# Two transformer layers on one core: who copies the finished attention products, and the order of the head groups

## The reference

```
q = split_heads(x @ Wq + bq); k = ...; v = ...        # (1, 16, 1024, 16) each
attn = einsum('bhqd,bhkd->bhqk', q, k) / sqrt(16)     # layer 0 adds a bias linear in the key's place
attn = where(causal, attn, min)
p = softmax(attn, axis=-1)
o = einsum('bhqk,bhkd->bhqd', p, v)                   # then o @ Wo, and the residual
```

## Time and profile before

| quantity | value |
|---|---|
| time, median of 3 runs | 471.26 us (470.86 to 472.94) |
| time of the profiled execution | 470.61 us |
| its span, first to last instruction | 468.9 us |
| mean granted TensorE clock | 0.989 of full speed |
| TensorE matmul busy | 432.2 us (92%) |
| VectorE busy | 313.2 us (67%) |
| ScalarE busy | 229.8 us (49%) |
| GpSimd busy | 159.5 us (34%) |

### The profile page before, as it was taken

How to read it: one execution, slowest core, us unless ns; L and a number is a source line. 1 busy time by engine, 2 the same in 40 slices (tenths; PEclk the granted TensorE clock), 3 DMA queues, 4 the chain that set the end, 5 groups by cost and what they waited for, 6 DMA issues and landing times.

```text
span 468.9 us, 7172 instructions
## 1 busy us (share of the span) xinstructions
PE 432.2 (92%) x2656; PEld 213.7 (46%) x2656; DVE 313.2 (67%) x624; ACT 229.8 (49%) x364; POOL 159.5 (34%) x228
## 2 busy tenths in 40 slices
PE   0899899999998989999999998999999998897997
PEld 0458643434433238434476464434333432174476
DVE  2576989998887028512234578899989882088883
ACT  2375554565666762321100552545566676824960
POOL 4168032302021121195950000333515336311780
PEclk9999999999999999999999997999999999999999
DMA  8899810000000000202000477200000000000002
GB/s 173 133 263 236 202 36 2 1 1 3 1 3 0 3 6 1 67 2 67 0 0 1 126 196 215 71 2 1 3 1 2 2 0 2 0 2 1 1 20 71
DMA packets 23894, 22.50 MB, mean 48 GB/s; under 512 B 5194, under 2 KB 23114, under 8 KB 23850
## 3 DMA queue, kind: packets, MB, share of 16 engines
q1 hardware_dynamic: 22132, 19.02, 16.9%
q0 software_dynamic: 608, 2.50, 2.1%
q10 hardware_dynamic: 1120, 0.53, 0.5%
HBM read 8.27 MB, written 1.05 MB: 20 GB/s over the span
## 4 chain that ended last, share of the span: by engine, by line
PE 73%; DVE 18%; ACT 4%; DMA 2%; issue 2%; POOL 1%; SPq 0%; ACTq 0%; DVEq 0%
PE ps L666 12%; PE ps L633 12%; DVE mx L1005 10%; PE ps L648 10%; PE ps L749 9%; PE ps L788 7%; PE ps L764 5%; PE ps L754 4%; PE ps L772 3%; ACT prob L901 3%; PE ps L574 3%; PE ps L636 3%; DMA x<-in_L_attn_x 2%; PE ps L583 1%; DVE stats L970 1%
## 5 line engine op out<-in xcount | busy, mean ns | idle before, releaser
L1005 DVE TENSOR_REDUCE mx<-ps 128x1 f32<-128x512 f32 (+3 forms) x304 | 183.7, 655 | 26.7 <-PE ps L636 20.4
L901 ACT ACTIVATE prob<-ps 128x1024 f32<-128x1024 f32 (+1 forms) x192 | 146.0, 809 | 96.8 <-PE ps L648 96.2
L633 PE MATMUL ps<-kS,qS 99*128 99x512 bf16 (+7 forms) x384 | 112.4, 335 | 5.0 <-DVE mx L1005 3.6
L489 POOL TENSOR_SCALAR_AFFINE_SELECT prob<-prob 128x256 f32<-128x256 f32 x128 | 52.2, 414 | 181.3 <-ACT prob L901 179.7
L648 PE MATMUL ps<-qS,kS 101*128 101x512 bf16 (+7 forms) x384 | 92.7, 329 | 2.2 <-ACT prob L901 1.9
L666 PE MATMUL ps<-prob,v 128*32 128x512 f32 (+3 forms) x768 | 81.9, 498 | 1.2 <-POOL prob L489 1.2
L633 PEld LDWEIGHTS ps<-kS,qS 99*128 99x128 bf16 (+1 forms) x384 | 36.0, 98 | 78.8 <-DVE mx L1005 59.8
L636 PE MATMUL ps<-mask_q,identb 128*128 128x128 bf16 x256 | 50.4, 225 | 0.0
L648 PEld LDWEIGHTS ps<-qS,kS 101*128 101x128 bf16 (+1 forms) x384 | 31.9, 98 | 40.3 <-ACT prob L901 19.5
L749 PE MATMUL ps<-xnT,gu0T 128*128 128x512 f32 (+1 forms) x96 | 42.2, 596 | 0.7 <-ACT xnT L827 0.7
L1028 DVE COPY oT<-ps 128x512 f32<-128x512 f32 x16 | 10.9, 682 | 37.3 <-PE ps L666 37.3
(11 more groups left out here) (125 smaller groups left out, 498.0 us busy)
## 6 DMA issues: line engine op xcount, KB each, us to landing
qS<-parts SPq DMA_DIRECT2D x24, 128.0 KB, 3.4
kS<-parts SPq DMA_DIRECT2D x24, 128.0 KB, 3.0
qS<-prob SPq DMA_DIRECT2D x12, 128.0 KB, 5.8
kS<-prob SPq DMA_DIRECT2D x12, 128.0 KB, 5.1
qS<-xn SPq DMA_DIRECT2D x12, 128.0 KB, 2.4
kS<-xn SPq DMA_DIRECT2D x12, 128.0 KB, 2.4
x<-in_L_attn_x SPq DMA_DIRECT2D x2, 512.0 KB, 7.6
out<-x SPq DMA_DIRECT2D x8, 128.0 KB, 1.7
```

The lines of the kernel that those rows point to most:

```text
L489: nc.gpsimd.affine_select(out=square, in_=square, compare_op=ALU.is_ge, fill=0.0, base=0, pattern=[[0, 2], [1, P]], channel_multiplier=-1) ...
L633: mmi = nc.tensor.matmul(span, qS[0:K_MAX[L], c, g * G + h, qt * P:(qt + 1) * P], kS[0:K_MAX[L], g * G + h, key0:key0 + keys], start=True, ...
L901: nc.scalar.activation(prob[:, n % 3, 2 * pair:2 * pair + 2, off:CH], ps[:, 2 * (m % 2):2 * (m % 2) + 2, off:CH], ACT.Exp, scale=SCALE).th ...
L1005: ins = nc.vector.tensor_reduce(mx[:, slot, qt, heads[0]:heads[-1] + 1, part], src, AX_X, ALU.max)
```

## The change

Two things are changed. The copy of a unit's finished products from `ps[:, 7]` to `oT` is taken out of VectorE's queue and put in ScalarE's. It stands there one step after the unit's last exponentials, that is, behind the exponentials of the first step of the next unit. The waits that belong to it (for the last product, and in layer 1 for `w8_round`) move along. And the list of units is another one: three chunk-0 units, then all four chunk-1 units, and the chunk-0 unit of the last group at the end.

```
-CGS = [(g, c) for c in range(NC) for g in range(NG)]
+CGS = [(0, 0), (1, 0), (2, 0), (0, 1), (1, 1), (2, 1), (3, 1), (3, 0)]
...
+                def take_o(s):
+
+                    cg = STEPS[s][0]
+                    if s == LAST_STEP[cg]:
+                        if L == 1 and cg == 0:
+                            act.wait_ge(w8_round, 2)
+                        act.wait_ge(pv_done, L * N_STEP + s + 1)
+                        g, c = CGS[cg]
+                        nc.scalar.copy(oT[:, g, c * CH:(c + 1) * CH], ps[:, 7]).then_inc(o_taken, 1)
+
                 for s in range(N_STEP):
...
+                    if s >= PV_LAG:
+                        take_o(s - PV_LAG)
+                for s in range(N_STEP - PV_LAG, N_STEP):
+                    take_o(s)
                 nc.scalar.activation(warm[:], nhalf[:, 0:1], ACT.Silu)
...
-                    elif entry[0] == "pv" and entry[1] == LAST_STEP[STEPS[entry[1]][0]]:
-                        cg = STEPS[entry[1]][0]
-                        if L == 1 and cg == 0:
-                            dve.wait_ge(w8_round, 2)
-                        dve.wait_ge(pv_done, L * N_STEP + entry[1] + 1)
-                        g, c = CGS[cg]
-                        nc.vector.tensor_copy(oT[:, g, c * CH:(c + 1) * CH], ps[:, 7]).then_inc(o_taken, 1)
```

## The result

The changed kernel takes 463.85 us (median of 6 runs, 461.9 to 465.55), the one before 471.4 us beside it on the same chip (470.56 to 476.57). The medians lie 7.6 us apart. The ratio, which is taken only from runs in the faster of the two states that runs of a program fall into, is 0.9834 with a 95% interval of 0.9805 to 0.9864: 1.7% faster, 7.8 us. I had forecast 468.0 us, in a range from 465.0 to 471.3.

What follows compares the result with a forecast made beforehand. VectorE was taken to bound the early chunk-0 windows, TensorE the dense chunk-1 ones, ScalarE's exponentials the last. Per layer +0.8 us ahead and -2.4 us after made -1.6, doubled -3.2: 468.0 us, range 465.0 to 471.3.

Steps and rivals of the forecast that it cites:

- the lead: Attention up to the end of unit 2: added VectorE work less two copies, +0.8 us per layer.
- Copies off VectorE, where VectorE ends last: From the copy of unit 0 to that of unit 2: two copies of 0.6 us come free, 1.2 us.
- Copies off VectorE, in the dense windows: TensorE-bound windows: gain bounded by 0 and 0.6 us each, taken as 0 since VectorE idles there.
- The new order ahead of the chunk-1 units: Up to the third unit's last product: 70 max items for 67, +1.8 us, and longer negation and wider items, +0.2.
- The middle: Windows 3 to 7 of a layer: 84.59 us before, 82.2 after, with three chunk-1 windows summing to 59.9.
- The end: End of a layer's attention: last copy 0.59 us for 0.69, counted as nothing; table load covered by 0.8 us.
- The third copy: Sign to look for in the profile after: the third copy of layer 0 near 88.4 us.
- The sum: Whole kernel: +0.8 and -2.4 make -1.6 us per layer, -3.2 us for two layers, so 468.0 us.
- A (eaten): Costlier lead, late ScalarE copies and longer chunk-1 windows leave -0.2 us per layer: 470.9 us, chance 0.20.
- C (slower): ScalarE's copy blocks the exponentials at unit boundaries, 0.9 us each, +2.9 us per layer: 477 us, chance 0.07.
- D: Output projections behind the attention: a clock dip in layer 1 too or longer in layer 0, 469.1 to 470.2 us, chance 0.06.
- B: VectorE no longer holds up max-item banks: dense windows give 0.3 us each, lead only 0.4; 465.5 us, chance 0.12.

Runs made afterwards that it cites:

- experiment 2: The kernel before with the new list of units, copies still on VectorE: 468.24 us (ratio 0.9934).
- Experiment 6: The changed kernel with four VectorE reductions made twice in window 4 of layer 0 and window 2 of layer 1: 466.7 us, one look.
- experiment 4: The changed kernel with every copy made twice on ScalarE: 469.97 us (ratio 0.9984).
- experiment 9: The changed kernel with two VectorE reductions made twice behind the first product of window 0, in both layers: 472.24 us, one look.
- experiment 10: The changed kernel measured once more, nothing altered: 462.99 us (ratio 0.9872).
- experiment 1: The changed kernel with the old list of units, so only the copies moved to ScalarE: 466.05 us (ratio 0.9889).

## Why the prediction was wrong in size

The step that failed is the charge for the lead: I took the three added max items at VectorE's full rate, +1.8 us, also the two of them that stand in window 0. In layer 0 they cost about 0.2 us there, not 1.2; in layer 1 the clock hides what they cost. The second error is the zero for the copies in the dense windows, which gave 0.7 us a layer. The paragraphs follow the terms of the sum.

*Copies off VectorE, where VectorE ends last (-1.2): right.* Windows 1 and 2 gave 0.60 and 0.56 us (experiment 2 against after).

*Copies off VectorE, in the dense windows (0): wrong.* I read "TensorE busy 19.80 of 19.80" as bound by TensorE alone. Windows 3 to 5 gave 0.30, 0.18 and 0.18, 0.66 us a layer. Experiment 6 shows why: in such a window VectorE's work counts at 0.70. The ends of matmuls in the profile are modelled and neighbours overlap, so a busy share of 100% can hide small waits for a free bank; the 5.9 us that the weight loads of max items waited for VectorE in such a window are not seen in it. The Trainium skill ("Perfetto Trace Analysis", section "Identifying the Most-Contended Engine") says that the busy share of matmuls is no good measure of how near TensorE is to its limit; experiment 6 agrees, with 1.67 us more in a window that had no idle time to show. At this rate a copy of 0.6 us is worth 0.4; experiment 4 puts the price of one on ScalarE at 0.15 there. By this estimate, which takes the rate of the burst for that of a single copy, 0.27 us should remain, and 0.18 to 0.30 did.

*The new order ahead of the chunk-1 units (+2.0, so +0.8 with the copies): this is the step that failed most.* The order alone cost +0.81 and +0.65 in windows 1 and 2. One item and the longer negation stand there, 0.8 us at VectorE's full rate, so that rate was right for them. But I charged it wherever an item stood, and the other two, 1.2 us, stand in window 0. Of these the one behind the first product cost nothing, and the one ahead of it about 0.2 us in layer 0 (experiment 9). There VectorE doesn't end last alone: behind the first product TensorE is busy 7.56 of 7.56 us, and 1.2 us of VectorE's work costs 0.6. In window 0 of layer 1 the order alone measured 23.10 for 23.22 us, but at another clock (0.93 for 0.85). With the copies, the windows 1 and 2 came out 0.35 us shorter than before in layer 0 and 0.50 in layer 1. With window 0 as the two profiles have it, the lead is +0.02 us in layer 0 (the end of unit 2 stands 35.79 us behind the last group of transposes L592, before 35.77) and -0.3 in layer 1. So the error is 0.8 and 1.1 us, the largest of the terms.

*The middle (84.59 to 82.2, -2.4): nearly right, in part by luck.* It became 82.04 from 84.73 us, -2.69, and -2.67 in layer 1. With the order alone the three dense windows took 60.27 us where I had 59.9, and the copies then took 0.66 off. The dense windows are 20.10, 19.84 and 19.67 us for 20.2, 20.2 and 19.5; unit 6 took 15.89 for 15.8, unit 7 6.54 for 6.5. In unit 6 I had 0.5 us for the copy and the three items together; it took 15.89 us with the order alone as well, so the copy was worth none of it. The turn of unit 7 no longer waits. This row of after answers to the earlier trace rows:

```profile
150.67 0.22 PE L695 MATMUL ps<-identb,mneg 128*32 128x128 bf16 x1
```

*The end: right but for 0.1 us.* The last copy is 0.1 us shorter, and I had counted nothing. The table load stayed covered, by 0.62 us for 0.8.

*The third copy* began at 86.21 us; I had 88.4. Of the difference 1.35 us is a start that came earlier in this execution (the last group of transposes L592 began at 49.73 us for 51.08), the rest, 0.8 us, is the term above.

*The sum.* Per layer the lead accounts for 0.8 to 1.1 us, the middle for 0.3 and the end for 0.1 of what was missing. The two layers give -6.2 us by the first two profiles (without window 0 of layer 0, which differs too much between executions), and -7.0 with the window 0 of layer 1 of experiment 10. The ratios make it 7.8 and 6.0 us, with intervals from 6.4 to 9.2 and from 3.9 to 8.2; the medians differ by 7.6 and 8.2. So the windows explain most of the gain. The rest, up to 2 us by the medians, I can't give to the change: layer 0's start and the clock differ by as much between executions of one kernel. Whether the change makes a late first transfer or a dip of the clock likelier or rarer is open.

*The rivals.* A (eaten) and C (slower) did not come. D's dip was in none of the three profiles of after, and in one of three of before; the rival had it come more often after the change. B came closest: its mechanism, that no copy holds up the banks of max items, is what experiments 1, 2 and 6 speak for, and its 465.5 us was the nearest number. Its sizes were less so: it had 0.9 us for the three dense windows, which gave 0.66, and a lead of +0.4. I gave it 0.12 because of the full busy share.

## What to carry to other kernels

A window in which the profile shows TensorE busy all the time may still pay for work taken off another engine; a few added instructions of known length on that engine give its rate, 0.5 to 0.95 in the four places here, and this is a better base for a forecast than a choice between 0 and 1. The same item of work cost 0.9 of itself or more in a window where VectorE ended last, and 0.7 of itself, half of itself or nothing beside other work: charge each by where it stands. Here it paid to run a short unit last, as the last one has nothing beside it to hide its waits.

## What was not expected

Windows 1 to 7 of the attention repeat within 0.03 us but for one, yet executions of one kernel differ by 4 us and more (before: 470.56 to 476.57). What differs between their profiles is above all the start of layer 0, where the first scores wait 0 to 3.4 us for a transfer of 8 KB behind pieces of 128 KB and the granted clock may then be 0.50 for 8 us. Then there are 0.8 us in window 0 of layer 1, and 1 to 1.5 us in an output projection or the last feed-forward (from layer 1's first gate matmul to the end it took 40.99 us in the first profile of before and 42.32 in the third). So differences of 1 or 2 us between kernels are better read from the same windows of two profiles than from the medians.
